# Attention output of a fused transformer-and-experts kernel: products folded over heads into 32-row bands, then one projection

## The reference

```
kv  = cumsum over tokens of  k[d] * vs[m]           (8 x 8 per head)
x_m = sum over d of  qs[d] * kv[d, m] * sink_alloc
attn = concat over heads(x) @ Wo + bo
h   = layernorm(inputs + attn)
out = layernorm(h + gelu(h @ W1 + b1) @ W2 + b2)
```

## Time and profile before

| | us |
|---|---|
| median of three runs | 427.27 (425.92 to 428.07) |
| the profiled execution, its own time | 425.98 |
| its span | 424.2 |
| TensorE busy | 374.6 (88%) |
| VectorE busy | 336.9 (79%) |
| GpSimd busy | 225.6 (53%) |
| ScalarE busy | 214.1 (50%) |

### The profile page before, as it was taken

One profiled execution on the slowest core, in us unless ns is written; L12 is line 12 of the kernel. 1 busy time (PEld: TensorE's weight loads), 2 busy tenths in 40 slices (PEclk: granted clock), 3 DMA queues, 4 the chain that ended last, 5 costly groups with the idle time before them and its releaser, 6 DMA issues.

```text
span 424.2 us, 6434 instructions
## 1 busy us (share of the span) xinstructions
PE 374.6 (88%) x2082; PEld 261.1 (62%) x2082; DVE 336.9 (79%) x795; ACT 214.1 (50%) x391; POOL 225.6 (53%) x263
## 2 busy tenths in 40 slices
PE   8897889788899999898979998998988998899991
PEld 3545655475647875586649773877468665775551
DVE  3559957597799898989799889988898979853632
ACT  2240234427654576627842784457652783275541
POOL 2016244963488329933794369733993379564111
PEclk9999999899999999999999999999999999999997
DMA  7235007200280007200450028000820054000000
GB/s 262 104 81 143 1 2 179 68 2 1 47 202 2 0 2 186 88 1 2 116 158 2 0 52 222 3 0 2 200 75 0 1 121 105 0 2 25 2 25 25
DMA packets 19857, 26.58 MB, mean 63 GB/s; under 512 B 1648, under 2 KB 9968, under 8 KB 19824
## 3 DMA queue, kind: packets, MB, share of 16 engines
q1 hardware_dynamic: 19680, 25.96, 23.6%
q10 hardware_dynamic: 144, 0.21, 0.2%
HBM read 7.29 MB, written 2.10 MB: 22 GB/s over the span
## 4 chain that ended last, share of the span: by engine, by line
DVE 32%; PE 30%; issue 17%; POOL 11%; DMA 4%; ACT 3%; SPq 1%; DVEq 0%; POOLq 0%; ACTq 0%
POOL prod L840 6%; DVE kv L1034 6%; DVE cum_kv L1040 5%; PE pY L507 4%; PE pB L353 4%; DMA vb<-vs 3%; PE pY L427 3%; PE pG L496 3%; PE pG L489 2%; DVE cum_ks L930 2%; DVE cum_q L930 2%; PE pG L483 2%; DVE gel L1131 2%; DVE delta L1093 2%; DVE stats L1050 2%
## 5 line engine op out<-in xcount | busy, mean ns | idle before, releaser
L840 POOL TENSOR_TENSOR prod<-cum_kv,q_fac 128x512 f32<-128x512 f32 x64 | 92.9, 1458 | 28.4 <-DVE cum_kv L1040 25.9
L403 PEld LDWEIGHTS pO<-s_wor,prod 128*128 128x128 f32 x512 | 62.3, 191 | 29.1 <-issue 15.3
L403 PE MATMUL pO<-s_wor,prod 128*128 128x128 f32 x512 | 68.0, 280 | 10.4 <-POOL prod L840 10.0
L1034 DVE TENSOR_TENSOR kv<-k,vb 128x512 f32<-128x512 f32 x64 | 54.0, 843 | 6.8 <-DMA vb<-vs 6.8
L827 POOL TENSOR_TENSOR var_eps<-mv,s_con 128x4 f32<-128x4 f32 x32 | 12.2, 382 | 73.4 <-DVE mv L1054 73.4
L1040 DVE TENSOR_TENSOR_SCAN cum_kv<-p_ones,cum_kv,kv 128x512 f32<-128x512 f32 x32 | 40.5, 1275 | 0.6
L1040 DVE TENSOR_TENSOR_SCAN cum_kv<-p_ones,kv 128x512 f32<-128x512 f32 x32 | 38.5, 1214 | 0.5
L507 PEld LDWEIGHTS pY<-s_moe,gel 128*128 128x128 f32 x256 | 31.1, 192 | 6.1 <-issue 4.3
L748 ACT ACTIVATE relu<-pG,s_att 128x512 f32<-128x512 f32 x28 | 19.1, 684 | 28.5 <-PE pG L489 28.5
L507 PE MATMUL pY<-s_moe,gel 128*128 128x128 f32 x256 | 32.6, 276 | 0.0
L830 POOL TENSOR_TENSOR rstd<-var_eps,s_con 128x4 f32<-128x4 f32 x32 | 32.4, 1013 | 0.0
(11 more groups left out here) (164 smaller groups left out, 790.5 us busy)
## 6 DMA issues: line engine op xcount, KB each, us to landing
vb<-vs SPq DMA_DIRECT2D x64, 256.0 KB, 4.5
xT<-x_t SPq DMA_DIRECT2D x8, 256.0 KB, 4.7
xt<-x SPq DMA_DIRECT2D x8, 256.0 KB, 4.8
out<-y SPq DMA_DIRECT2D x8, 256.0 KB, 2.3
s_moe<-moe_w SPq DMA_DIRECT2D x1, 836.0 KB, 10.1
s_wor<-wo_rep SPq DMA_DIRECT2D x1, 512.0 KB, 8.0
s_ffn<-ffn_w SPq DMA_DIRECT2D x1, 512.0 KB, 8.6
s_con<-consts SPq DMA_DIRECT2D x1, 502.0 KB, 4.6
```

The lines of the kernel that those rows point to most:

```text
L403: mm = pe.matmul(pO3[:, s, :], prod[:, m % 4, s * P:(s + 1) * P], s_wor[:, m, :], start=False, stop=(m == DH - 1), skip_group_check=True)
L840: pool.tensor_tensor(prod[:, m % 4, :], cum_kv[t.par][:, m, :], q_fac[t.par][:, :], ALU.mult).then_inc(prod_ready, 1)
L1034: dve.tensor_tensor(kv[:, m % 3, :], k[t.par][:, :], vb[:, m, :], ALU.mult).then_inc(kv_ready, 1)
```

## The change

The sum over d and the projection are taken apart. The stationary operand of the new `fold_heads` is a 128x32 matrix of zeros and ones; the moving one is `prod` of m with its 512 tokens. It sums the eight partitions of each head. The features m and m + 4 share one band of 32 rows in `pY`: m mod 4 gives the band, and the half (m < 4 or not) selects which 16 of its rows get the head sums. Two features are folded per call, when both products are there. When all eight are folded, ScalarE copies `pY` to `attT` in SBUF, and `attn_out` adds its product with Wo, whose rows are reordered to match, onto `pO`, in four matmuls of 128 columns.

TensorE's order changes with it: no fold at the end of a step, pair 0 after `project_k`, pair 1 after the transposes of x2, pairs 2 and 3 after the logits, then `project_v(a)`, `attn_out(b)` and `expert_out(d, 0)`. `expert_out` waits for the copy, since it writes the same bank, and the first fold waits until the FFN's output has been read from it. ScalarE's copy stands behind `x2T_out`, and `v_out` now precedes `gate_exp`. VectorE's statistics wait for `attn_out`. `keep_busy` calls of the second step move, and write to `pG[1]`. The weights of the fold (`s_fold`, 192 columns) replace `s_wor` (1024 columns) in the same load. GpSimd's program has no edit of its own; its products still wait for `red_ready`, which each fold now raises.

```diff
-            def reduce_out(t, m):
-                if m == 0:
-                    pe.wait_ge(xseed_ready, t.n + 1)
-                pe.wait_ge(prod_ready, DH * t.n + m + 1)
+            def fold_heads(t, pair):
+                if pair == 0:
+                    wait(pe, norm_ready[1], SUB * t.n)
+                pe.wait_ge(prod_ready, DH * t.n + 2 * pair + 2)
+                for m in (2 * pair, 2 * pair + 1):
+                    j, half = m % 4, m // 4
+                    pe.matmul(pY[32 * j:32 * j + 32, :], s_fold[:, 32 * half:32 * half + 32], prod[:, j, :],
+                              start=(half == 0), stop=(half == 1), skip_group_check=True).then_inc(red_ready, 1)
+
+            def attn_out(t):
+                pe.wait_ge(xseed_ready, t.n + 1)
+                pe.wait_ge(attT_ready, t.n + 1)
                 for s in range(SUB):
-                    mm = pe.matmul(pO3[:, s, :], prod[:, m % 4, s * P:(s + 1) * P], s_wor[:, m, :],
-                                   start=False, stop=(m == DH - 1), skip_group_check=True)
-                mm.then_inc(red_ready, 1)
+                    mm = pe.matmul(pO3[:, s, :], attT[:, s * P:(s + 1) * P], s_fold[:, 64:64 + P],
+                                   start=False, stop=True, skip_group_check=True)
+                mm.then_inc(attn_done, 1)
...
                 if f == 0:
+                    if t.plus(2).exists():
+                        pe.wait_ge(attT_ready, t.n + 3)
...
             def second_step(b):
                 a = b.plus(1)
-                keep_busy(2)
-                for m in range(1, 5):
-                    reduce_out(b, m)
+                pe.wait_ge(y_free[0], 16)
+                keep_busy(3, pG[1])
+                fold_heads(b, 0)
+                keep_busy(2, pG[1])
+                fold_heads(b, 1)
                 head_sums(a, 0, True); head_sums(a, 0, False); project_v(a)
-                keep_busy(1)
-                reduce_out(b, 5)
+                keep_busy(1, pG[1])
                 denominators_T(a, 0); denominators_T(a, 1)
-                keep_busy(1)
-                reduce_out(b, 6)
+                fold_heads(b, 2)
+                keep_busy(2, pG[1])
                 head_sums(a, 1, True)
-                keep_busy(1)
+                keep_busy(1, pG[1])
                 head_sums(a, 1, False)
-                keep_busy(1)
-                reduce_out(b, 7)
-                keep_busy(2)
+                keep_busy(1, pG[1])
+                fold_heads(b, 3)
+                keep_busy(1, pG[1])
+                attn_out(b)
+                keep_busy(1, pG[1])
                 cumulate_e(a)
...
-                if B: reduce_out(b, 1)
                 if A: project_k(a)
+                if B: fold_heads(b, 0)
                 if D: inter2(d, 2); inter2(d, 3)
-                if B: reduce_out(b, 2)
                 if s.n == 1: keep_busy(1, pM)
                 if C: x2_T(c)
-                if B: reduce_out(b, 3); reduce_out(b, 4)
+                if B: fold_heads(b, 1)
                 if C: logits(c)
-                if B: reduce_out(b, 5); reduce_out(b, 6); reduce_out(b, 7)
+                if B: fold_heads(b, 2); fold_heads(b, 3)
+                if A: project_v(a)
+                if B: attn_out(b)
                 if D: expert_out(d, 0)
-                if A: head_sums(a, 0, True); head_sums(a, 0, False); project_v(a)
+                if A: head_sums(a, 0, True); head_sums(a, 0, False)
...
-                if A: reduce_out(a, 0)
...
+            def attT_out(t):
+                act.wait_ge(red_ready, DH * (t.n + 1))
+                wait(act, attn_done, t.n)
+                act.activation(attT[:, :], pY[:, :], ACT.Copy).then_inc(attT_ready, 1)
...
-                if C: normalise(c, 2); x2T_out(c); gate_exp(c)
-                if A: v_out(a); spread_denominators(a, 0)
+                if C: normalise(c, 2); x2T_out(c)
+                if B: attT_out(b)
+                if A: v_out(a)
+                if C: gate_exp(c)
+                if A: spread_denominators(a, 0)
...
                 if i == 0:
-                    dve.wait_ge(red_ready, DH * (t.n + 1))
+                    dve.wait_ge(attn_done, t.n + 1)
```

More of the change, by code:

```diff
@@ L63, in run_steps, with build @@
         step(Tile(n))
-def build(nc, x, x_t, att_w, consts, wo_rep, rows, gate_row, ffn_w, moe_w, out):
+def build(nc, x, x_t, att_w, consts, fold_w, rows, gate_row, ffn_w, moe_w, out):
     ctx = ExitStack()
@@ L80, in build @@
         s_con = sb("s_con", [P, 1004])
-        s_wor = sb("s_wor", [P, DH, P])
+        s_fold = sb("s_fold", [P, 2 * 32 + P])
         s_row = sb("s_row", [P, 7, P])
@@ L151, in build @@
         prod = sb("prod", [P, 4, TOK])
+        attT = sb("attT", [P, TOK])
         x_bo = sb("x_bo", [P, SUB, P])
@@ L253, in build @@
         po_written = sem("po_written")
+        attT_ready, attn_done = sem("attT_ready"), sem("attn_done")
         xseed_ready, hseed_ready = sem("xseed_ready"), sem("hseed_ready")
@@ L302, in _ @@
             load_xt(Tile(0))
-            sp.dma_start(s_wor[:, :, :], wo_rep).then_inc(y_free[0], 16)
+            sp.dma_start(s_fold[:, :], fold_w).then_inc(y_free[0], 16)
             sp.dma_start(s_ffn[:, :], ffn_w).then_inc(y_free[1], 16)
@@ L545, in opening @@
                 keep_busy(4)
-                pe.wait_ge(y_free[0], 16)
-                reduce_out(a, 0)
             def second_step(b):
                 a = b.plus(1)
-                keep_busy(2)
-                for m in range(1, 5):
-                    reduce_out(b, m)
+                pe.wait_ge(y_free[0], 16)
[3 more added lines that the diff above has]
+                fold_heads(b, 1)
                 head_sums(a, 0, True); head_sums(a, 0, False); project_v(a)
-                keep_busy(1)
-                reduce_out(b, 5)
+                keep_busy(1, pG[1])
                 denominators_T(a, 0); denominators_T(a, 1)
-                keep_busy(1)
-                reduce_out(b, 6)
+                fold_heads(b, 2)
+                keep_busy(2, pG[1])
                 head_sums(a, 1, True)
-                keep_busy(1)
+                keep_busy(1, pG[1])
                 head_sums(a, 1, False)
-                keep_busy(1)
-                reduce_out(b, 7)
-                keep_busy(2)
+                keep_busy(1, pG[1])
[3 more added lines that the diff above has]
+                keep_busy(1, pG[1])
                 cumulate_e(a)
-                keep_busy(2)
+                keep_busy(2, pG[1])
                 h_T(b); compensation_T(a); factor_T(a)
@@ L768, in second_step @@
                 source_exp(a); alloc_tanh(a)
-                normalise(b, 0)
+                attT_out(b); normalise(b, 0)
                 spread_scale(a, False); spread_scale(a, True)
@@ L1267 @@
                              np.full((P, SUB), -1.0)], axis=1).astype(np.float32)
-    wo_rep = np.repeat(a["Wo"].reshape(HEADS, 1, DH, P), DH, axis=1).reshape(P, DH, P)
+    none = np.zeros_like(headsum)
+    wo = a["Wo"].reshape(HEADS, 2, 4, P).transpose(2, 1, 0, 3).reshape(P, P)
+    fold_w = np.concatenate([headsum, none, none, headsum, wo], axis=1)
     rows = np.stack([a["bo"], a["ln1_g"], a["ln1_b"], a["b2"], a["ln2_g"], a["ln2_b"], m["bo"]])
@@ L1278 @@
                             m["lora_B"].transpose(0, 2, 1).reshape(P, FF), pieces(m["wo"].T)], axis=1)
-    arrays = {"x": x, "x_t": x.T, "att_w": att_w, "consts": consts, "wo_rep": wo_rep, "rows": rows,
+    arrays = {"x": x, "x_t": x.T, "att_w": att_w, "consts": consts, "fold_w": fold_w, "rows": rows,
               "gate_row": gate_row, "ffn_w": ffn_w, "moe_w": moe_w}
```

## The result

The changed kernel takes 437.59 us (median of 4 runs, 437.19 to 438.73), the kernel before 427.32 beside it: ratio 1.0254, 95% interval 1.0234 to 1.0275. It is slower by 2.5%; the forecast was 438.2. The profiled execution has a span of 435.7 us against 424.2, that is 11.5 more. Of one later run, b1, the profiled execution took 2122 us where its five others took 429 to 431; it is left out there and its trace is not read.

A forecast was written before the change was run, and what follows sets the result against it. No engine alone was taken as the bound: the step is a relay between engines. Terms of 2.4 (second step), 1.9 (step 1), 5.5 (middle) and 2.4 (last) made 12.2 us on 425.98: 438.2 us, range 432 to 442.

The forecast's parts named there:

- That TensorE's sum is not what decides, but where the work stands: Per tile, TensorE's work goes from 7.1 to 7.8 us, saving nothing; the place of the new work decides.
- The unit price of a fold (0.86, a pair 1.72): Each 512-column fold on TensorE costs what any 512-column matmul costs, 0.86 us, so a pair takes 1.72.
- The rival of overlapping bands: Folds in neighbouring bands overlap on TensorE, a pair taking 1.29 us; 8.1 us slower in sum, 434.1; chance 0.24.
- Middle steps, 5 x 1.1: Steps 2 to 6: head sums 1.48 us late, 0.37 regained, transposes 1.1 late; 5.5 us in all.
- the rival "absorbed": Middle steps absorb the delay because VectorE's gate work fills the wait before q_sink; 6.7 us remain, 432.7; chance 0.08.
- The end of a step "gains nothing": Product 0's reduction (0.89 us) leaves the step's end; no gain, as TensorE then waits for xT anyway.
- The clock of 1.00: Granted clock read as 1.00 in both stretches of the profile before, so durations needed no correction.
- Step 1, +1.9: Fold pair 3, projection and output matmuls delay head sums from 93.72 to 95.63; no slack at the transposes: +1.9 us.
- Second and last step, +2.4 each: From product 7 to the statistics, 3.6 us in place of 1.20, through fold pair, copy and output matmuls.
- Cover for the copy, the table load and the pY wait: Value projection hides the copy (0.85 us), the exponential table load finishes in time, waits on pY cost nothing.
- product 4 is not held up: GpSimd's product 4 starts about 221.4, after pair 0's first fold is out at 221.0; no cost taken.
- Changes of kind cost a tail: Six changes between folds and wide matmuls, 0.17 us each, drain TensorE; +5, 443.2 us; chance 0.08.

The follow-up runs named there:

- b1: Kernel before the change, with only reduction 0 moved from the end of a step to behind the next step's wait for xT: 429.73 us, ratio 1.007.
- a4: Changed kernel with both folds of a pair written to the same 32-row band: 443.59 us, ratio 1.0392.
- a6: Changed kernel with filler matmuls in all idle stretches of TensorE (at xT, before step 1's x2 transposes, between fold pairs 2 and 3): 434.18 us, ratio 1.0166.
- b3: Kernel before, with reduction 0 moved behind the wait for xT and one filler matmul in the place it left: 428.89 us, ratio 1.0052.
- a7: Changed kernel with fillers in all TensorE idle stretches and the next tile's head sums ahead of expert piece 0: 433.74 us, ratio 1.0146.
- a9: a6 with output matmuls reading a constant tile, so that they wait for no ScalarE copy: 430.84 us, ratio 1.0097.
- a3: Changed kernel with the next tile's head sums put ahead of expert piece 0, no fillers added: 435.45 us, ratio 1.0192.
- a1: Changed kernel with two filler matmuls where TensorE waits for xT in steps 2 to 6: 436.19 us, ratio 1.0201.
- d1: Kernel before, with value projection ahead of head sums, expert piece 0 behind them, piece 2 behind the first denominators' transposes: 423.75 us, ratio 0.9948.

## Why the prediction was right in its time, and where it was wrong

The path was right and the closeness of the time was luck: one cost in the sum was much too large (1.72 for 0.98), and another was missing.

*That TensorE's sum is not what decides, but where the work stands:* right. TensorE's busy time fell by 6 us and the kernel became 10 us slower.

*The unit price of a fold (0.86, a pair 1.72):* wrong, and it is the step of the forecast that failed first. A pair takes 0.98. The rival of overlapping bands had the mechanism, and its price (1.29) was still too high: both halves run beside their neighbours', two slots and a little. a4 shows that the cause is the bands. Put into the forecast's own sum, 0.98 in place of 1.72 makes 1.7 at each end, 1.2 in step 1 and 0.2 in a middle step, 5.6 in all; with the clock held the traces show 5.2. So the hand-overs were priced well, and this term carries nearly all that was too much. The trace agrees here with the Trainium skill ("TensorE: Matmul & The Clock Gate", Part 3: Packing small matmuls), which has matmuls on different strips run concurrently; here two of them go from 1.90 to 1.05.

*Middle steps, 5 x 1.1:* wrong in size. With pairs at 0.98 and the clock held they come out at nothing (a6, -0.06 to 0.13 each). The late head sums are there, 0.66 us of them where the chain had 1.48 (0.6 with the cheaper pair). What they cost is made up by a shorter wait ahead of `q_sink` and by a stall of VectorE that went elsewhere, which the chain did not have. That is the result of the rival "absorbed", though not by its reason: the gate work does not fill the wait. The 2.8 us that the middle steps did cost came from half clock.

*The end of a step "gains nothing":* true, and not the whole of it. I priced the missing reduction by what it freed, and never asked what it had done: it kept TensorE at work until 1.4 to 2.1 us before xT landed (steps 3 to 6). Without it the waits are 2.7 to 3.8 us in steps 3 to 6, and in the profiled execution the granted clock falls behind each of them. b1 shows the price with no other edit, and b3 shows the falls. The forecast took the clock of 1.00 from the rows of before and assumed it for after; that is the sentence that hid 6 us.

*Step 1, +1.9:* 3.96. Without the fall at 93 us it is 1.15 (a6), as the cheap pair makes it. The other 2.8 are the half clock from 93 us on, where folds and less work leave TensorE idle for 2.38 us before pair 3 and 2.79 before the x2 transposes.

*Second and last step, +2.4 each:* mechanism and place right. 2.15 and 2.57 measured. From fold to statistics it is 3.03 in the second, not 3.6, the pair being cheaper, and 3.75 in the last, where half clock adds 0.8 to the output matmuls. With the clock held the last step costs 1.9 (a7). The copy's 0.85 is confirmed at both ends (a9).

*Cover for the copy, the table load and the pY wait:* right in steps 1 to 6; a9 finds 0.1 at most there. The forecast that product 4 is not held up was right by its margin only at full clock: at half clock it waits 2.46 us.

*Changes of kind cost a tail:* not seen. The next matmul starts 0.98 behind a pair's first, whether it has 128 columns or 512, 0.12 over two slots, and if that is the price of the two changes it is below the 0.17 allowed for each. (This rival's own 443.2 lay outside the stated range, which was said to take in most of it.)

So 438.2 was near 437.6 because two errors met: about 7 us too much, nearly all of it from the price of a pair, and about 6 us missing for the clock. The sign and the idea that product 7's way is the price stand; the sizes do not.

## What to carry to other kernels

Work that fills a wait is not free to remove: ask of each matmul taken away what TensorE's idle time before its next wait becomes, and look at the granted clock behind waits of that length in every trace that you have. Matmuls of 32 output rows cost about half here when neighbours write different 32-row bands, but an extra hand-over through another engine costs its full length wherever nothing independent stands beside it, so fold in the middle of a pipeline and not at its ends. And look at small operations with long durations: a 0.18 us operation that took 1.18 stood behind GpSimd, and moving one expert piece, which let it start first, brought more here than the rebuilt reduction.

## What the runs showed of the hardware

Two matmuls of 128x32 weights and 512 columns in f32 take 1.05 us on different 32-row bands of one bank and 1.90 on the same band.

Waits of TensorE of 2.7 to 3.8 us ahead of xT were followed by half clock in steps 3 to 6 of the changed kernel. The length of the wait does not decide it alone. In a3 the clock stayed at 1.00 behind waits of 3.00 and 2.76 us and fell behind 3.47 and 3.24; it fell behind 1.86 in a1; and 2.13 went both ways (no fall at 218.26 before, a fall at 219.42 in b3).

```profile
176.50:179.50 3.00, 0.00 (x1) 0.00 (x0) 2.96 (x12) 0.31 (x1) 2.85 (x3) 1.00 0.84 238
179.50:183.00 3.50, 3.50 (x10) 1.18 (x11) 3.50 (x4) 2.33 (x5) 3.36 (x6) 1.00 0.29 74
```

(a3, the wait of 3.00 us and the work behind it.) Executions of a3 lie up to 5.5 us apart, the longest with the lowest mean clock (0.956). That the places where the clock falls make this spread is likely and not shown, as one execution of each kernel was traced.

A VectorE operation of 128x32 elements took 0.18 us when it started ahead of GpSimd's 1.28 us `h_res` and up to 1.18 when it started behind it, until that ended; the prefix sum that starts with `h_res` in d1 (235.09) took its usual 1.28. The Trainium skill ("SBUF — State Buffer", SBUF: two separate sides) says that a VectorE operation with two SBUF inputs and a GpSimd operation that reads SBUF exclude each other for a whole instruction. The trace agrees for VectorE: the gate operation has two such inputs, and so has the `kq` of a6 that took 1.32. The prefix sum has one, as it reads its ones from a PSUM bank (`p_ones`): in the kernel before, the 57 prefix sums of `kv` that started while GpSimd was at work took 1.19 to 1.29 us, the seven others 1.21 to 1.28.
